# Attention inside a transformer block: value matmuls in groups of 3, 3, 2, 3, 3 and 2 key tiles instead of eight pairs, with VectorE's small operations at other steps

## What is computed

```python
def reference(x, qkvw, qkvb, ow, ob, A_w, B_w, Wq_w, keys):
    xn = layernorm(x)                                  # x: 2048 x 1024, f32
    q, k, v = split_heads(xn @ qkvw + qkvb)            # 32 heads of 32 columns
    probs = softmax(q @ k.T / sqrt(32), axis=-1)       # 2048 x 2048 for each head
    attn = merge_heads(probs @ v) @ ow + ob
    gate = top16_softmax_gate(xn @ Wq_w.T @ keys.T)    # 64 experts of rank 8
    z = (xn @ A_w.T) * gate
    return x + attn + 2.0 * (z @ B_w.T)
```

## Time and profile before

| | |
|---|---|
| median of three runs | 2524.45 us (2520.17 to 2524.98) |
| the profiled execution | 2530.7 us |
| its span, from first to last instruction | 2528.9 us |
| mean granted TensorE clock | 0.994 of full speed |
| TensorE matmuls busy | 2489.5 us, 98% |
| VectorE busy | 1493.7 us, 59% |
| ScalarE busy | 1224.9 us, 48% |
| GpSimd busy | 1636.1 us, 65% |

### The profile page before, as it was taken

How to read it: one execution, slowest core, us unless ns; L and a number is a source line. 1 busy time by engine, 2 the same in 40 slices (tenths; PEclk the granted TensorE clock), 3 DMA queues, 4 the chain that set the end, 5 groups by cost and what they waited for, 6 DMA issues and landing times. The chain is left out here.

```text
span 2528.9 us, 34185 instructions
## 1 busy us (share of the span) xinstructions
PE 2489.5 (98%) x12856; PEld 1622.4 (64%) x12856; DVE 1493.7 (59%) x2524; ACT 1224.9 (48%) x2311; POOL 1636.1 (65%) x556
## 2 busy tenths in 40 slices
PE   7999999999999999999999999999999999989999
PEld 4788888888755555555555555555555555448887
DVE  7511110104588788788888788878888888522221
ACT  5211111110066676667666666667666766761000
POOL 0110111221079999999999999999999999962121
PEclk9999999999999999999999999999999999999999
DMA  4233335324367777777877877877777777564332
GB/s 167 92 125 124 124 115 162 102 79 125 96 158 164 150 160 165 158 151 165 165 150 158 165 153 155 167 150 161 164 159 150 166 165 151 116 158 141 116 104 88
DMA packets 174991, 359.26 MB, mean 142 GB/s; under 512 B 90432, under 2 KB 115520, under 8 KB 143808
## 3 DMA queue, kind: packets, MB, share of 16 engines
q0 software_dynamic: 22752, 165.69, 33.2%
q1 hardware_dynamic: 152096, 191.70, 26.5%
HBM read 127.42 MB, written 63.70 MB: 76 GB/s over the span
## 5 line engine op out<-in xcount | busy, mean ns | idle before, releaser
L1173 DVE TENSOR_REDUCE part_max<-ps_b 128x1 f32<-128x512 f32 x1984 | 1214.4, 681 | 263.7 <-PE ps_b L1046 263.6
L997 POOL TENSOR_TENSOR psum_p<-psum_p,probs 128x2048 f32<-128x2048 f32 x253 | 1181.8, 4671 | 53.6 <-ACT probs L1159 43.3
L1159 ACT ACTIVATE probs<-ps_b 128x512 f32<-128x512 f32 x1920 | 971.2, 621 | 351.2 <-PE ps_b L1036 345.9
L1036 PE MATMUL ps_b<-q,k 97*128 97x512 f32 x1344 | 547.6, 412 | 0.0
L1046 PE MATMUL ps_b<-k,q 96*128 96x512 f32 x1344 | 536.8, 401 | 0.6
L1036 PEld LDWEIGHTS ps_b<-q,k 97*128 97x128 f32 x1344 | 252.4, 188 | 223.4 <-issue 135.8
L1064 PE MATMUL ps_b<-probs,v 128*32 128x512 f32 x2640 | 319.4, 598 | 0.5 <-ACT probs L1159 0.5
L351 POOL TENSOR_TENSOR wlo<-wraw,whi 128x1024 fp32r<-128x1024 f32 x20 | 48.0, 2399 | 405.7 <-ACT whi L512 405.7
L1036 PE MATMUL ps_b<-qk 97*128 97x512 f32 x704 | 289.8, 414 | 2.0 <-PEq L84 1.7
L1046 PEld LDWEIGHTS ps_b<-k,q 96*128 96x128 f32 x1344 | 256.4, 191 | 49.5 <-DVE part_max L1173 17.9
L1046 PE MATMUL ps_b<-qk 96*128 96x512 f32 x640 | 254.8, 398 | 0.0
(11 more groups left out here) (128 smaller groups left out, 2572.6 us busy)
## 6 DMA issues: line engine op xcount, KB each, us to landing
psum_q<-probs POOLq DMA_DIRECT2D x158, 1024.0 KB, 7.7
qk<-qk_scr SPq DMA_DIRECT2D x66, 256.0 KB, 7.3
qk_scr<-ehi SPq DMA_DIRECT2D x16, 1024.0 KB, 3.9
qk_scr<-elo SPq DMA_DIRECT2D x16, 1024.0 KB, 6.7
k<-qk_scr SPq DMA_DIRECT2D x63, 256.0 KB, 4.1
q<-qk_scr SPq DMA_DIRECT2D x63, 256.0 KB, 8.0
wraw<-wcat SPq DMA_DIRECT2D x21, 512.5 KB, 7.4
craw<-cz_scr SPq DMA_DIRECT2D x14, 768.0 KB, 4.8
```

Of the source, the lines that this page charges most:

```text
L997: pool.tensor_tensor(acc[:, :], first[:, :], tile(h, t)[:, :], ALU.add).then_inc(pool_done, 1)
L1036: pe.matmul(ps[:, st_bank(n), :], kp[s][0:PACK + 1, t * P:(t + 1) * P], qp[s][0:PACK + 1, b * NQ:(b + 1) * NQ], start=True, stop=True).the ...
L1159: act.activation(tile(h, t)[:, b * NQ:(b + 1) * NQ], ps[:, st_bank(n), :], ACT.Exp, scale=SCALE).then_inc(exp_done, 1)
L1173: dve.tensor_reduce(part_max[hn % 2][:, tn, b:b + 1], ps[:, ring_bank(u), :], AX_X, ALU.max) \
```

## The change

Value matmuls come in other groups. In heads 0 to 30, tiles 0, 1, 2 follow step 3, tiles 3, 4, 5 step 6, tiles 6, 7 step 8, tiles 8, 9, 10 step 11, tiles 11, 12, 13 step 14, and tiles 14, 15 step 0 of the next head: six groups where there were eight. Head 31 keeps its pairs. From head 1 on, steps 3 and 14 carry three maxima instead of four and steps 7 and 15 five; where a step carries five, the first is issued ahead of the step's first transposed score. The reciprocal moves from step 9 to 11, the transpose of the row maxima with its negation from step 13 to 12 (not in head 0), and SyncE's load of the queries for head h + 2 waits for three value tiles of head h instead of four.

```diff
--- before.py
+++ after.py
@@ -60,9 +60,11 @@
 SLOTS = 3
 RING = 8
 LEAD = 4
-TRANSPOSED_AT = TT - LEAD + 1
+VALUES_AT = {0: (14, 15), 3: (0, 1, 2), 6: (3, 4, 5), 8: (6, 7), 11: (8, 9, 10), 14: (11, 12, 13)}
+LAST_VALUES_AT = {0: (14, 15), **{t: (t - 2, t - 1) for t in range(2, TT, 2)}}
+MAXIMA_AT = {3: 3, 7: 5, 14: 3, 15: 5}
 WIDE_FROM = (HEADS - 2, TT - LEAD)
-SUMS_AT, RECIPROCAL_AT = 6, 9
+SUMS_AT, RECIPROCAL_AT = 6, 11
 
 OUT_KT = KT + Z_BLOCKS
 READY_KT = OUT_KT - 1
@@ -794,8 +796,13 @@
             if h == 0:
                 first, count = (6 * (t - 1), 6) if t < 6 else (30 + 5 * (t - 6), 5)
                 return [(1 + n // 64, n // QB % TT, n % QB) for n in range(first, first + count)] if t else []
-            hn, tn = (h + 1, t + LEAD) if t + LEAD < TT else (h + 2, t + LEAD - TT)
-            return [(hn, tn, b) for b in range(QB)] if hn < HEADS else []
+            first = QB * (TT * h + LEAD) + sum(MAXIMA_AT.get(i, QB) for i in range(t))
+            every = [(1 + n // (QB * TT), n // QB % TT, n % QB) for n in range(first, first + MAXIMA_AT.get(t, QB))]
+            return [u for u in every if u[0] < HEADS]
+
+        def transposed_at(h):
+
+            return TT - LEAD + (1 if h == 0 else 0)
 
         ring_order = []
         for h in range(HEADS):
@@ -803,7 +810,7 @@
                 ring_order += [("max", *u) for u in maxima_at(h, t)]
                 if t == SUMS_AT and h >= 1:
                     ring_order.append(("sum", h - 1, 0, 0))
-                if t == TRANSPOSED_AT and h < LAST:
+                if t == transposed_at(h) and h < LAST:
                     ring_order.append(("flip", h + 1, 0, 0))
         ring_order.append(("sum", LAST, 0, 0))
         ring_place = {u: n for n, u in enumerate(ring_order)}
@@ -958,7 +965,7 @@
                     if h == LAST:
                         load_ready_rows()
                     if h + 2 < HEADS:
-                        sp.wait_ge(pv_done, TT * h + 4)
+                        sp.wait_ge(pv_done, TT * h + 3)
                         load_queries(h + 2)
                     invert_sums(h - 1)
                     if h + 2 < HEADS:
@@ -1088,21 +1095,26 @@
 
             def step(h, t):
                 ahead = maxima_at(h, t)
+                lead, ahead = (ahead[:-QB], ahead[-QB:]) if h >= 1 else ([], ahead)
+                for u in lead:
+                    scores(*u)
                 for b in range(QB):
                     scores_t(h, t, b)
                     for u in ahead[b:b + 1]:
                         scores(*u)
                 for u in ahead[QB:]:
                     scores(*u)
-                if t == 0 and h >= 1:
-                    values(h - 1, TT - 2)
-                    values(h - 1, TT - 1)
-                if t % 2 == 0 and t >= 2:
-                    values(h, t - 2)
-                    values(h, t - 1)
+                taken = (LAST_VALUES_AT if h == LAST else VALUES_AT).get(t, ())
+                if t == 0:
+                    if h >= 1:
+                        for tp in taken:
+                            values(h - 1, tp)
+                else:
+                    for tp in taken:
+                        values(h, tp)
                     if h == LAST:
-                        last_sums(t - 2)
-                        last_sums(t - 1)
+                        for tp in taken:
+                            last_sums(tp)
                 if t == SUMS_AT and h >= 1:
                     sums(h - 1)
 
```

## The result

The changed kernel takes 2635.72 us in the median of four runs (2630.1 to 2641.47), the one before 2524.56 (2520.17 to 2524.98, four runs). The ratio is 1.0439, with a 95% interval of 1.0418 to 1.0460: slower by 4.4%, 111 us. The direction was forecast, the size was not: 10 us had been predicted, and 2635.72 lies far above the range of 2527 to 2542. The profiled execution took 2633.04 us, 102.3 more than the one before.

The account below looks back on a forecast made before the run. TensorE's queue was taken as the bound, each value group lasting as long as its scores or maxima, whichever is more. 7.9 (29 heads) + 1.84 + 0.47 = +10.2 us on 2524.45 gave 2534.7 us, range 2527 to 2542.

Parts of the forecast that it names:

- The 0.34 for a switch: TensorE going over to values and back costs 0.34 us a group; two switches less save 0.68 a head.
- 0.86 for a tile: One value tile of four matmuls takes TensorE 0.86 us.
- 0.234 for a score: TensorE's score matmuls start 0.234 us apart.
- its pace of 0.487: ScalarE's exponentials come 0.487 us apart, each giving back a bank; at most 0.05 late in twelve-maximum groups, inside VectorE's 0.33.
- The line 0.80 + 0.60 for each maximum: Length in us of a value group that VectorE paces, plus 0.86 for a third tile; predicted 48.64 a head.
- the 2 to 3 forecast: Scores' weight loads (line of the maxima) wait 2 to 3 us a head for VectorE, up from some 0.5.
- Head 0 +1.84: Head 0, paced by VectorE: seven groups' 0.80 (5.60) become five plus four third tiles (7.44), +1.84 us.
- Head 30 +0.47: Head 30, without maxima from step 12: first group to the one at step 14 grows from 40.82 to 41.29 us.
- The moved work, costed at nothing: Moved reciprocal, SyncE's transfers behind it, queries' load and GpSimd's added 0.25 us were all said to delay nothing.
- Rivals: VectorE keeps up, faster (about 2507, 0.08); waits partly swallowed, no change (2523, 0.14); ScalarE held up, slower still (0.08).
- The third, slower still: Exponentials in groups of twelve more than 0.53 us apart; at 0.55, +23 and about 2557 us; chance 0.08.

Follow-up runs that it names:

- e7: e2's kernel with VectorE reducing only 256 of 512 columns in each reduction: 2523.13 us, ratio 0.9997 to the kernel before.
- e8: The kernel before with VectorE reducing only 256 of 512 columns in each reduction: 2514.93 us, ratio 0.9965.
- e2: The changed kernel with SyncE's load of the negated maxima issued right after the reciprocals' write, ahead of their reads and the load of values: 2530.15 us, ratio 1.0031.
- e6: The changed kernel with only the value groups changed; maxima, reciprocal, transpose and queries' load as in the kernel before: 2563.64 us, ratio 1.0155.
- e4: The kernel before, value matmuls in pairs, with only the reciprocal moved from step 9 to 11: 2659.59 us, ratio 1.0538.
- e10: e4's kernel with e2's order in SyncE's queue: 2521.0 us, ratio 0.9994 to the kernel before.
- e9: The changed kernel with the 256 KB load of values behind the load of the negated maxima in SyncE's queue: 2538.62 us, ratio 1.0075.

## Why the prediction was right in direction and wrong in size

- *The 0.34 for a switch, 0.86 for a tile, 0.234 for a score*: right within 0.1 us a head. Two switches would be 0.68, e7 against e8 has 0.57. In e7 the scores' weight loads wait for ScalarE 59.0 us over 1400 (14.2 before), so its pace of 0.487 may hold the longer groups up a little there; no run separates that.
- *The line 0.80 + 0.60 for each maximum, taken from head 0*: right in every group of the changed kernel, to 0.01 us. It gave 48.64 a head; e2 has 48.59 to 48.66 in all 29. It was 0.3 short for one group of e6, that of twelve maxima with the transpose. The weight loads of the maxima wait 56.7 us for VectorE in e2 over 1400, 2.0 a head, at the lower end of the 2 to 3 forecast.
- *Head 0 +1.84*: from VectorE's first maximum to the first copy of the sums are 78.25 us (698.74 to 776.99) instead of 76.68 (698.42 to 775.10), +1.57. In e2 the same stretch is 77.23, so this term is borne out to about 1 us only. *Head 30 +0.47*: 42.1 against 41.55 in e2, +0.55; in the changed kernel itself that interval is 49.94, since the stall strikes there too.
- *The moved work, costed at nothing*: this is the step that failed; it cost some 92 us. The text saw that the reciprocal's write, its four reads and the load of values move some 4 us back, and that the load of the negated maxima is behind them in SyncE's queue. It then said that this load "waits for the negation about 2.4 us into the next group and has a whole group until the head's first score". Three things were not worked out. The write itself was taken at the 1.4 us that it has in the trace of the kernel before, though at its new place it runs beside a 1 MB transfer, and took 5.1. (That trace had a warning: its first load of negated maxima, 8 KB issued 2.45 us behind such a transfer, took 4.6 us to land, the others 1.8 to 3.5.) The queue's delay was never added up to the time of issue: reciprocal at 1508.92, +0.3, +5.1, four reads 1.8, values 0.4 to 1.4, makes 1517, not 1513.3. And what the load itself would run beside there was not asked: the load of values in front of it, and GpSimd's next transfer, which goes out at 1517.29. How little time is left shows in the short head: landed at 1571.96 + 3.2 = 1575.2, TensorE there at 1575.9, hence 0.7 us. Everything beyond this is a stall, and the stall of 3.8 us shown above cost its head 6.5, since the clock was at half behind it.
- *Rivals*: none of the three was this one. The third, slower still, had the size in view (+23) but another place, ScalarE; its exponentials are no further apart than before.
- *The sum*: of the 102.3 us between the two profiled executions, 7.4 in the full heads (at 48.62) and 1.9 up to the first copy of the sums are of the kind that was forecast; 84.4 are the full heads' excess over 48.62, 8.4 come in the interval from head 30 to 31 (0.55 of it in e2 too), and 0.2 behind it. The direction wasn't luck: e2 shows the forecast mechanism alone slower by 7.8 us. But it is a tenth of what was measured.

The Trainium skill (DMA: Bandwidth & Descriptors, Queues, rings and completion order) says that a DMA engine takes turns between its queues after each packet. By it alone a small load would wait for a packet or so in front of it and not for a transfer. Here 8 KB took 1.8 us in most heads of the kernel before and 6.4 to 8.3 in the changed kernel when issued just behind 1 MB. No run shows which part of that is the turns, which the load of values in front, and which the number of pieces that the 8 KB are cut into.

## What to carry to other kernels

When an operation is moved, redo the timetable of every queue that its result passes through, with landing times from rows where the same neighbours were in flight, down to the last thing queued behind it: here moving an operation of 0.25 us, on an engine with 9 us to spare a head, cost 5.4%. Ahead of a load with a deadline nothing belongs that waits for another transfer, and no larger load that isn't needed sooner; its place in the queue was worth 0.04 (changed kernel against e2) to 0.05 (e4 against e10) of the kernel's time, with nothing computed differently. An experiment that changes an order moves two things: name both before it runs. A group's length as the longer of two lines, one read from a stretch of the same trace where the other engine is the pace, predicted each group of the changed kernel to a hundredth of a microsecond.

## What the runs showed of the hardware

- An 8 KB load landed in 1.8 us in 24 of 29 heads of the kernel before. In the changed kernel, with a 256 KB load in front of it in the queue, it took 2.8 to 4.1 when issued 0.5 to 0.9 us ahead of a 1 MB accumulating transfer, and 6.4 to 8.3 when issued up to 0.7 behind it. Without the 256 KB in front (e9) it took 1.8 to 1.9 even 0.07 to 0.37 ahead. In e4 five of 16 took 6.3 to 9.0 at 0.8 to 0.9 ahead, for a reason that no run shows.
- A write of 8 KB took 1.4 us in the kernel before and 5.1 when issued 2 us behind a 1 MB transfer (changed kernel).
- TensorE's clock was granted at 0.50 behind an idle stretch of 3.8 us and was at 1.00 again from 1530.5, after 6 us of matmuls; this stall cost its head 6.5 us.
- The changed kernel's heads don't settle: one comes out at 48.6 us and the next at 55, where its load goes out a few tenths of a microsecond later against the transfer. Its runs lie 11 us apart, those of the kernel before 5, with all full heads at 48.3 to 48.5.
